# Column maxima across four partition groups: eight small reduces in place of two transposes

## The reference

```python
a = layer_norm(audio_kv, gamma, beta)
Q, K, V = heads(x @ Wq.T), heads(a @ Wk.T), heads(a @ Wv.T)
scores = where(mask, einsum('bhtd,bhsd->bhts', Q, K) * 64 ** -0.5, -inf)
attn = softmax(scores, axis=-1)
out = einsum('bhts,bhsd->bhtd', attn, V) @ Wo.T
return x + tanh(gate) * out
```

## Time and profile before

| | us |
|---|---|
| median of 3 runs | 2176.8 (2169.89 to 2179.46) |
| the profiled execution, its own time | 2173.98 |
| its span, first to last instruction | 2172.2 |
| TensorE busy, matmuls | 2048.7 |
| VectorE busy | 1724.8 |
| GpSimd busy | 1491.7 |
| ScalarE busy | 1122.0 |

### The profile page before, as it was taken

The page is one execution under the profiler, slowest core; times in us unless marked ns, Lnnn a source line. Parts: engine busy times, 40 slices in busy tenths (PEclk is TensorE's granted clock), DMA queues, the critical chain, the costliest instruction groups (busy, mean ns, idle before and its releaser), DMA issues.

```text
span 2172.2 us, 29043 instructions
## 1 busy us (share of the span) xinstructions
PE 2048.7 (94%) x8960; PEld 1595.3 (73%) x8960; DVE 1724.8 (79%) x2257; ACT 1122.0 (52%) x1578; POOL 1491.7 (69%) x809
## 2 busy tenths in 40 slices
PE   6899789999999999999999999999999999999996
PEld 4677567777677777777777777777777777777774
DVE  7676677878877888788787887877888788887875
ACT  5555464454644555454645456444465454654542
POOL 6878796566856578656776668656686657856564
PEclk9999999999999999999999999999999999999997
DMA  6465544543335533544435543445433544335331
GB/s 258 150 235 197 185 144 140 206 168 136 137 120 205 175 129 122 186 168 159 146 104 192 185 158 106 149 176 176 165 111 132 219 153 150 137 119 175 137 118 60
DMA packets 137175, 341.59 MB, mean 157 GB/s; under 512 B 56576, under 2 KB 57600, under 8 KB 136192
## 3 DMA queue, kind: packets, MB, share of 16 engines
q1 hardware_dynamic: 137088, 340.33, 44.7%
HBM read 288.89 MB, written 51.38 MB: 157 GB/s over the span
## 4 chain that ended last, share of the span: by engine, by line
PE 69%; DVE 13%; POOL 8%; issue 5%; ACT 2%; DMA 2%; SPq 0%; DVEq 0%; POOLq 0%; ACTq 0%
PE pj L438 12%; PE pj L442 12%; PE pj L440 11%; PE sc L390 5%; PE sc L357 5%; PE sc L394 5%; PE sc L358 4%; PE sc L391 4%; DVE prob L719 4%; PE pv L382 3%; PE pv L383 3%; DVE m_b L713 2%; POOL p_lo L925 2%; POOL prob L929 2%; POOL w_lo L920 2%
## 5 line engine op out<-in xcount | busy, mean ns | idle before, releaser
L925 POOL TENSOR_TENSOR p_lo<-prob,p_hi 128x1024 fp32r<-128x1024 f32 x256 | 613.4, 2407 | 247.9 <-ACT p_hi L552 247.3
L694 DVE TRANSPOSE_TENSOR_REDUCE mq<-sc 128x32 f32<-128x1024 f32 x256 | 304.7, 1228 | 155.3 <-PE sc L358 155.1
L442 PE MATMUL pj<-a_hi,w_lo 128*128 128x512 f32 x1024 | 406.1, 397 | 0.0
L438 PE MATMUL pj<-a_hi,w_hi 128*128 128x512 f32 x1024 | 400.5, 391 | 5.6 <-issue 2.7
L440 PE MATMUL pj<-a_lo,w_hi 128*128 128x512 f32 x1024 | 405.2, 396 | 0.0
L764 DVE SCALAR_TENSOR_TENSOR xy<-sc,tg_b,xy 128x1024 f32 (+1 forms) x256 | 321.2, 1272 | 55.7 <-PE sc L394 51.9
L571 ACT COPY o_tmp<-pv 64x512 f32<-64x512 f32 x128 | 74.3, 580 | 562.4 <-PE pv L383 562.3
L936 POOL TENSOR_TENSOR r_b<-o,r_b 128x512 f32<-128x512 f32 x64 | 83.3, 1301 | 344.5 <-DVE r_b L736 344.5
L929 POOL TENSOR_TENSOR prob<-prob 128x1024 f32<-128x1024 f32 x128 | 308.0, 2407 | 0.0
L719 DVE TENSOR_TENSOR prob<-sc,m_b 128x1024 f32<-128x1024 f32 x256 | 301.3, 1218 | 4.4
L547 ACT ACTIVATE prob<-prob 128x1024 f32<-128x1024 f32 x256 | 271.7, 1061 | 5.6 <-DVE prob L719 3.2
(11 more groups left out here) (88 smaller groups left out, 3871.1 us busy)
## 6 DMA issues: line engine op xcount, KB each, us to landing
w_hi<-kept_hi SPq DMA_DIRECT2D x225, 512.0 KB, 3.7
w_lo<-kept_lo SPq DMA_DIRECT2D x225, 512.0 KB, 4.6
cx<-in_ctx SPq DMA_DIRECT2D x32, 512.0 KB, 5.7
xy<-in_xT SPq DMA_DIRECT2D x32, 512.0 KB, 6.6
kept_hi<-w_hi SPq DMA_DIRECT2D x32, 512.0 KB, 5.2
kept_lo<-w_lo SPq DMA_DIRECT2D x32, 512.0 KB, 6.2
out_y<-xy SPq DMA_DIRECT2D x7, 2048.0 KB, 9.2
w_raw<-in_wq SPq DMA_DIRECT2D x8, 512.0 KB, 4.2
```

The costliest lines, as they stand in the source:

```text
L438: pe.matmul(dst[:, 0], w_hi[:, w, cols], s_hi[:, i], start=i == 0, stop=False)
L442: mm = pe.matmul(dst[:, 0], w_lo[:, w, cols], s_hi[:, i], start=False, stop=i == KT - 1)
L694: dve.tensor_reduce(out=mq[:, 2 * i:2 * i + 2], in_=sc[:, 2 * i:2 * i + 2].rearrange("p s (b j) -> p s b j", j=32), op=ALU.max, axis=mybir ...
L925: pool.tensor_tensor(p_lo[:, 2 * i:2 * i + 2], prob[:, h, 2 * i:2 * i + 2], f32(p_hi[:, 2 * i:2 * i + 2]), ALU.subtract).then_inc(pl_done, 1)
```

## The change: eight reduces, and what moves with them

`group_maxima` is now first: four reduces, each over the four banks of one partition group of `mq`, all writing to partitions 0 to 31 of `m_four`. `key_maxima` then reduces over these four, four times, each writing the same result to another partition group of `m_all`. `spread_maxima` reads `m_all` from SBUF. All are on VectorE.

```diff
-FILL = ((5, 5, 2, 2, 2, 20), (5, 5, 2, 2, 2, 20))
+FILL = ((5, 4, 6, 2, 19), (5, 4, 7, 2, 18))
...
 # TensorE: maxima_turned and maxima_back are gone; their wait for o_add moves
             def values(k, h, i):
-                if i == 0 and h == 0:
-                    pe.wait_ge(vl_done, k + 1)
+                if i == 0:
+                    ge(pe, oadd_done, k * 2 + h - 1)
+                    if h == 0:
+                        pe.wait_ge(vl_done, k + 1)
...
                         values(*before, 0)
-                    maxima_turned(k, h)
                     take(stream, f[1])
-                    maxima_back(k, h)
-                    take(stream, f[2])
                     if started:
                         values(*before, 1)
                     if h == 0:
                         turn_v(k)
-                    take(stream, f[3])
+                    take(stream, f[2])
                     out_step(k, h, 0, kind)
...
 # VectorE
+            def group_maxima(k, h):
+                dve.wait_ge(mq_done, k * 4 + 2 * h + 2)
+                for c in range(4):
+                    dve.tensor_reduce(out=m_four[:, c], in_=mq[groups[c]].rearrange("p s b -> p b s"), op=ALU.max,
+                                      axis=mybir.AxisListType.X).then_inc(mg_done, 1)
+
             def key_maxima(k, h):
-                (one reduce of mq over the four banks into m_cols[:, 0:16])
+                dve.wait_ge(mg_done, k * 8 + 4 * h + 4)
+                for g in range(4):
+                    dve.tensor_reduce(out=m_all[groups[g]], in_=m_four[:].rearrange("p c b -> p b c"), op=ALU.max,
+                                      axis=mybir.AxisListType.X).then_inc(ma_done, 1)
...
             def spread_maxima(k, h):
-                dve.wait_ge(mt_done, k * 2 + h + 1)
+                dve.wait_ge(ma_done, k * 8 + 4 * h + 4)
                 dve.transpose(m_b[:].rearrange("p (b i) -> p b i", i=32),
-                              pv[h][:, 0, P:P + 16].rearrange("p (b o) -> p b o", o=1).to_broadcast((P, 16, 32))
-                              ).then_inc(mb_done, 1)
+                              m_all[:].rearrange("p (b o) -> p b o", o=1).to_broadcast((P, 16, 32))).then_inc(mb_done, 1)
...
 # VectorE, body
                 block_maxima(k, 0, 1)
+                group_maxima(k, 0)
                 key_maxima(k, 0)
-                group_maxima(k, 0)
...
                 if begun:
+                    o_add(k - 1, 0)
                     o_add(k - 1, 1)
...
                 block_maxima(k, 1, 1)
-                key_maxima(k, 1)
                 if not last:
                     q_low(k, 1)
                 group_maxima(k, 1)
+                key_maxima(k, 1)
...
-                o_add(k, 0)
                 column_sums(k, 0)
```

More of the change, by code:

```diff
@@ L67, in xattn_kernel @@
         m_b, r_b = sb("m_b", [P, T]), sb("r_b", [P, T])
-        mq, m_cols, m_rows = sb("mq", [P, TB, 16]), sb("m_cols", [P, P]), sb("m_rows", [P, 4, 32])
-        m_two = sb("m_two", [P, 64])
+        mq, m_four, m_all = sb("mq", [P, TB, 16]), sb("m_four", [32, 4, 16]), sb("m_all", [P, 16])
         rq, r_four = sb("rq", [P, 2, 16]), sb("r_four", [P, 4, 16])
@@ L96, in xattn_kernel @@
         init_done, row_done, mask_done, mrow_done = sem("init_done"), sem("row_done"), sem("mask_done"), sem("mrow_done")
-        mq_done, mc_done, mg_done, mr_done, mb_done, sub_done = (
-            sem("mq_done"), sem("mc_done"), sem("mg_done"), sem("mr_done"), sem("mb_done"), sem("sub_done"))
+        mq_done, mg_done, ma_done, mb_done, sub_done = (
+            sem("mq_done"), sem("mg_done"), sem("ma_done"), sem("mb_done"), sem("sub_done"))
         rq_done, rsum_done, rinv_done, rb_done = sem("rq_done"), sem("rsum_done"), sem("rinv_done"), sem("rb_done")
@@ L131, in xattn_kernel @@
         halves = (slice(0, HD), slice(HD, P))
+        groups = [slice(32 * g, 32 * (g + 1)) for g in range(4)]
         def splits(b, kind, pair):
@@ L359, in scores @@
                     mm.then_inc(s_done, 1)
[L361 to L368, removed]
             def turn_v(k):
@@ L471, in body @@
                         pe.wait_ge(mrow_done, 2)
-                        pe.wait_ge(init_done, 7)
+                        pe.wait_ge(init_done, 5)
                     if j == 0 and h == 0 and not (isinstance(k, int) and k == 0):
@@ L493, in body @@
                         turn_ctx(k, b, 4 * h + 1)
-                    take(stream, f[4] if kind != "prepare" else f[4] + 4)
+                    take(stream, f[3] if kind != "prepare" else f[3] + 4)
                     out_step(k, h, 1, kind)
@@ L498, in body @@
                         turn_ctx(k, b, 4 * h + 3)
-                    take(stream, f[5] if kind != "prepare" else f[5] - 4)
+                    take(stream, f[4] if kind != "prepare" else f[4] - 4)
             def drain():
@@ L675, in _ @@
             act.copy(w_hi[:, WV], w_raw[:, 0]).then_inc(whi_done, 1)
-            act.wait_ge(init_done, 7)
+            act.wait_ge(init_done, 5)
             mask_rows(-1, -1)
@@ L869, in drain @@
                 column_sums(LAST, 1)
+                o_add(LAST, 0)
                 o_add(LAST, 1)
@@ L875, in drain @@
                     accumulate(k, 2, n, n, n % 2, (B - 1) % 2)
-            dve.memset(m_cols[:], 0.0).then_inc(init_done, 1)
-            dve.memset(m_rows[:], 0.0).then_inc(init_done, 1)
             dve.memset(masked[:], MASKED).then_inc(init_done, 1)
```

12 lines of the change are left out of this document (1 added, 11 removed).

## The result

The changed kernel takes **2251.1 us** (median; 2250.0 to 2252.0) against 2176.9 us in the same job: ratio 1.0346, 95% interval 1.0322 to 1.0370. It is slower, as forecast, but by 74 us where the sum had 40, and outside the range (2172 to 2236). The profiled span grew from 2172.2 to 2249.5 us, by 77.3.

A forecast was written before the change was run, and what follows sets the result against it. TensorE sets the pace (busy 94%, 69% of the chain), waiting in each half for VectorE's chain up to the first subtraction. Terms 25 + 2 - 1 + 14 = +40 us on 2174 gave 2214 us, range 2172 to 2236.

The forecast's parts named there:

- The added chain: VectorE, maxima's end to m_b: eight reduces, each with a 0.03 us gap, take 2.35 us (bounds 1.73 to 2.51).
- the reduces overlap: Rival, eight reduces on VectorE: they overlap by 0.07, maxima to m_b takes 1.73 us, kernel 2132 us; chance 0.07.
- shorter reduces: Rival, VectorE: 32-partition reduces take 0.21 to 0.22 us each, kernel 2158 to 2171 us, about no change; chance 0.10.
- Odd half +0.41: Odd half of a pair: m_b 0.86 us later, two matmuls take 0.45 off the tail; +25 over 62 halves.
- Even half "-0.02: nothing": Even half of a pair: chain grows 0.29 us, one matmul moved ahead takes 0.23 off the tail; net nothing.
- o_add moved, +14 us: Head 0's o_add moved to the next pair's first half: late only in three special halves per batch, 1.94 x 7.
- At nothing: Items costed at zero: two memsets less at the start, values()'s waits on oadd_done, values() moved 0.9 us earlier.
- The clock in the new wait: Rival, odd half: clock falls in TensorE's wait of about 1.2 us, 62 x 1.5 = +93, 2307 us; chance 0.04.

The follow-up runs named there:

- e7: Changed kernel with all eight reduces reading and writing partitions 0 to 31 alone, the combination across groups left out: 2158.3 us (0.9909).
- e14: Changed kernel with the output step's wait for VectorE's subtraction put behind its long-satisfied waits instead of ahead of them: 2248.5 us (1.0325).
- e6: Changed kernel with o_add of head 0 put back at the end of its own pair: 2241.0 us (1.0289).
- e11: Kernel before with twelve satisfied waits ahead of each pair's maxima inside VectorE's loop over batches, making it 426 instructions: 2204.2 us (1.0113).
- e9: Kernel before with 30 satisfied waits in the first batch, shifting VectorE's loop over batches to 373 to 724: 15 us slower.
- e10: Kernel before with 128 satisfied waits in the first batch, shifting VectorE's loop over batches to 471 to 822: no slower.
- e13: Changed kernel with VectorE's loop over batches written out six times: 2225.3 us (1.0219).
- e8: Changed kernel with more fill matmuls ahead of the output step, FILL (5,4,9,2,16), (5,4,13,2,12): 2189.5 us (1.0055).
- e1: Changed kernel with 120 satisfied waits ahead of VectorE's first row statistics, shifting its loop to 539 to 965: 2260.9 us (1.0382).
- e5: Changed kernel with 192 satisfied waits among the first batch's maxima, shifting VectorE's loop to 611 to 1037: 2250.2 us (1.0340).

## Why the prediction was wrong

The direction was right, and so was the mechanism for ordinary pairs; a term of 33 us was not in the sum.

- *The added chain* (8 reduces with a gap each, 2.35 us): right, 2.36 and 3.05 measured, and e7 shows that the gaps, not the count, carry the loss (2158 us without the change of partitions, stalls included). The rival "the reduces overlap" names what happens in e7: 1.66 us where it said 1.73, and about 2132 us without the stalls where it said 2132. (Its 1.73 does not come out of its own terms: with 0.07 of overlap the eight give 1.55 if all overlap, 1.75 if six do. That the time agrees so closely is luck.) In the change itself it has no place, nor has "shorter reduces": they take 0.255 us on average at 32 partitions, as the rows with the same strides said.
- *Odd half +0.41*: +0.45 measured.
- *Even half "-0.02: nothing"*: +0.16, some 5 us in sum. The 0.40 us between subtraction and L391 was read from the odd half and set for both; in the even half two more waits stand behind the one that comes last, 0.09 us (e14). The rows of before have 0.48 us there (985.68 to 986.16), which could have warned, but not decided it, since TensorE did not wait there before. The other 0.07 is tail: 7.34 us from L385 to the next scores, where 7.50 less one matmul gives 7.27.
- *o_add moved, +14 us*: the special halves came out otherwise one by one (statistics odd +0.08 over an ordinary one instead of +0.47, prepare even +0.82 for 0.62, switch even +1.07 for 0.85, switch odd -0.56). With o_add back (e6) the statistics odd half is +0.43 and the switch odd half -0.46, nearly as after, so the move is not what made these two come out lower; why they did is open. In the prepare pair nmean against GpSimd's addition costs 0.56, and three more falls of the clock lie in the mean. e6 puts the move at 10 us. Together the statistics, prepare and switch pairs came to +14.0 us where the terms gave 19.1. These 5 us too many and the even halves' 5.6 too few offset each other, which is luck; batch 0 (+1.9), the ordinary odd halves (+1.3) and the rest (+1.4) make up the difference of 5 that is left.
- *"At nothing"*: here is the step that failed. The sum counted instructions by their time on the engine alone. The change makes VectorE's loop over batches 75 instructions longer, and after each of its five jumps back VectorE now stands idle before it goes on, which makes a half 6.6 us longer on average. e11 shows that the length makes the stall, e9 and e10 that the place does too, e13 that without the jump it is gone; that the idle time is the loading of instructions is argued, from these and from q14's packets. Without the jump the kernel took 2225.3 us (e13), 11 above the forecast of 2214 and inside its range.
- *The clock in the new wait*: did not fall in the odd half (1.00 in all 37 ordinary ones). But it fell in two places that the rival did not name: in all five stalled halves, where 9.9 of the 33 us are matmuls at the lower clock, and in all six prepare pairs instead of three.

No rival ended where the result did. The one for the clock (2307 us) was the only one above it, so the range's upper edge had nothing but the forecast's own spread behind it.

## What to carry to other kernels

Count a change's instructions as code too: in these runs a loop of VectorE that grew or moved stalled at each jump back, and TensorE, idle meanwhile, often came back at the lower clock; look at the instruction queue's packets and at waits on "issue" at a loop's head, and write out a loop that runs only a few times. Chains of small VectorE instructions cost their partition changes: plan them so that neighbours start on the same partitions. Before judging a change to a chain, retune what lies on either side of its wait in both versions: here three matmuls moved in the kernel before bring more than the change does at its best.

## What the runs showed of the hardware

- VectorE's loop over batches jumps back without a stall at 343 to 694, 453 to 804 and 471 to 822, and stalls at 373 to 724, 543 to 894 and in all four cases with 426 or 427 instructions. VectorE is idle at such a jump for 2.7 us (e8) to 5.3 us (e1). Without stalls the queue carries 21 or 22 packets of 8 KB, with them 46 to 53. Three pieces of 128 instructions explain all nine cases and the packets, six pieces of 64 the cases alone; that the hardware is built so is not shown, nor where the pieces begin.
- The granted clock fell to 0.50 at 617.0, after TensorE had been idle since 614, and rose again at 623.8. At that level matmuls start 0.43 us apart in place of 0.23.
- The Trainium skill, "Runtime: NRT & Kernel Launch", section "Instruction fetch mechanics", has the mechanism: a taken branch to a place outside the two loaded pages forces a fetch before work goes on. The runs agree with that, but not with a window of two pages of 256 instructions (e5, e9, e11).
- VectorE's reduce of 32 x 64 numbers takes 0.255 us and follows 0.18 us after the last one's start on the same partitions, 0.29 on others.
- Two satisfied waits behind a late one cost TensorE 0.09 us (0.49 against 0.40 in e14).
- nmean on 128 x 4 numbers takes 0.46 us as a median before and 1.02 after, and in both ends with GpSimd's running instruction.
